# Counting stage of a graph kernel: TensorE reads the one-hot where VectorE wrote it, without ScalarE's copy to columns-first

## The reference, cut to what matters

```python
x = _layernorm(x + _L0_gnn_ref(x, edge_index, 6250), axis=-1)
x = _layernorm(x + _L1_gnn_ref(x, edge_index, edge_attr_40, edge_weight, ...), axis=-1)

# layer 0
row, col = edge_index with a self loop for each node
deg = segment_sum(ones, row)
norm = deg_inv_sqrt[row] * deg_inv_sqrt[col]
out = segment_sum(label_mat[row] * norm[:, None], col)

# layer 1
gate = silu(edge_attr @ W1.T + b1) @ W2.T + b2 + adapt_logit
msg = gate * h[dst] * (cw * node_mult[dst])[:, None]
agg = segment_sum(msg, src) / clip(segment_sum(node_mult[dst], src))
```

## Time and profile before

| | before |
|---|---|
| median of 3 runs | 3051.34 us (3043.43 to 3051.47) |
| the profiled execution's own time | 3027.21 us |
| its span, first to last instruction | 3025.4 us |
| mean granted TensorE clock | 0.850 |
| busy: TensorE matmul, VectorE, ScalarE, GpSimd | 74%, 79%, 46%, 70% |
| ScalarE's copy `by_col<-oh_hi` (L323) | x101, 178.7 us, mean 1794 ns |

### The profile page before, as it was taken

One profiled execution on the slowest core, in us unless ns is written; L12 is line 12 of the kernel. 1 busy time (PEld: TensorE's weight loads), 2 busy tenths in 40 slices (PEclk: granted clock), 3 DMA queues, 4 the chain that ended last, 5 costly groups with the idle time before them and its releaser, 6 DMA issues. The chain is left out here.

```text
span 3025.4 us, 73628 instructions
## 1 busy us (share of the span) xinstructions
PE 2250.1 (74%) x25909; PEld 1913.9 (63%) x25909; DVE 2404.3 (79%) x5424; ACT 1395.5 (46%) x2929; POOL 2121.9 (70%) x1852
## 2 busy tenths in 40 slices
PE   6980476678777787777787877787878787788475
PEld 5760365566666666655666666676767666667475
DVE  9994577777787777877788897888888878887698
ACT  7982244444444444444444444444444444445123
POOL 7506777877777777777777777777777777760165
PEclk9765688888888888988888898888989888979797
DMA  8405233333433434333344454444444444442896
GB/s 322 148 2 163 62 112 108 101 126 116 127 113 115 127 115 124 117 112 112 118 148 153 143 155 146 147 145 145 145 147 147 144 144 145 156 138 103 333 389 224
DMA packets 174987, 441.53 MB, mean 146 GB/s; under 512 B 92662, under 2 KB 92662, under 8 KB 154806
## 3 DMA queue, kind: packets, MB, share of 16 engines
q1 hardware_dynamic: 103754, 236.05, 23.4%
q0 software_dynamic: 67888, 194.98, 20.7%
q10 hardware_dynamic: 3004, 5.90, 0.6%
HBM read 292.51 MB, written 144.27 MB: 144 GB/s over the span
## 5 line engine op out<-in xcount | busy, mean ns | idle before, releaser
L722 POOL DMA_INDIRECT slot<-table,gidx x1616 | 1811.9, 1121 | 633.6 <-issue 620.2
L821 PEld LDWEIGHTS route<-parts,oh_r 128*128 128x128 bf16 x11312 | 764.9, 100 | 91.6 <-issue 66.9
L821 PE MATMUL route<-parts,oh_r 128*128 128x148 bf16 x11312 | 812.9, 232 | 3.2 <-DVE parts L1224 3.0
L1089 DVE TENSOR_SCALAR oh_r<-iota_r,spot 128x896 bf16<-128x896 f16 x1616 | 613.5, 451 | 74.4 <-PE route L821 74.4
L894 ACT ACTIVATE routed<-route 128x444 bf16<-128x444 f32 (+1 forms) x1010 | 507.9, 513 | 258.5 <-PE route L821 240.0
L856 PE MATMUL pwin<-slot,oh_d 128*128 128x144 bf16 x1616 | 167.6, 276 | 404.2 <-DMA slot<-table,gidx 372.1
L856 PEld LDWEIGHTS pwin<-slot,oh_d 128*128 128x128 bf16 x1616 | 147.8, 155 | 428.2 <-issue 270.0
L777 PEld LDWEIGHTS pwin<-win,oh_t 128*128 128x128 bf16 x4848 | 262.3, 117 | 200.6 <-issue 101.8
L777 PE MATMUL pwin<-win,oh_t 128*128 128x80 bf16 (+1 forms) x4848 | 277.0, 227 | 77.1 <-ACT ssum L904 71.6
L747 PE MATMUL phid<-attr,w 80*96 80x512 f32 x404 | 282.2, 789 | 44.4 <-issue 44.1
L1195 DVE TENSOR_TENSOR prod<-slot,got 128x256 f32<-128x256 f32 x202 | 84.6, 419 | 231.3 <-ACT parts L955 231.2
(11 more groups left out here) (228 smaller groups left out, 3257.3 us busy)
## 6 DMA issues: line engine op xcount, KB each, us to landing
rows<-slots SPq DMA_DIRECT2D x51, 1295.0 KB, 8.8
oh_t<-dst_row SPq DMA_DIRECT2D x101, 512.0 KB
erows<-slots SPq DMA_DIRECT2D x51, 777.0 KB
attr<-in_edge_attr SPq DMA_DIRECT2D x101, 320.0 KB
slots<-zeros SPq DMA_DIRECT2D x53, 518.0 KB
slot<-table,gidx POOLq DMA_INDIRECT x1616
table<-tab SPq DMA_DIRECT2D x3, 676.0 KB, 5.9
weight_t<-weights SPq DMA_DIRECT2D x101, 8.0 KB
```

What stands on the lines that cost most here:

```text
L722: e.indirect_dma_start(out=slot[:, s, g, :], out_offset=None, in_=table0, in_offset=bass.IndirectOffsetOnAxis(ap=gidx[:, s, g:g + 1], axis ...
L821: mm = e.matmul(route[:, (NPH * m + phase) % 2, RC * (j - a):RC * (j - a + 1)], oh_r[:, c, slot_of, :], parts[:, s % 2, c, :], start=(c == ...
L1089: oh = e.tensor_scalar(oh_r[:, c], iota_r[:, :, :], spot[:, s % 2, c:c + 1], None, ALU.is_equal)
```

## The change

`by_col`, its semaphore `laid` and ScalarE's step `lay` go. TensorE's step `count` waits for VectorE's `oh_ready` (both one-hots of the tile) and takes its moving operands from `oh_hi` itself: 51 columns with a step of 16 elements for `deg`, and for `tot` four runs of 52 columns, each with a step of 16 elements. The values that enter each sum are the same, and so are the outputs.

```diff
@@ ScalarE
-                    def lay(i, s):
-                        t = U * i + s
-                        e.wait_ge(oh_ready, 2 * (t + 1))
-                        if since(i, s, OR):
-                            e.wait_ge(oh_used, t - OR + 2)
-                        e.activation(by_col[:, s % OR], oh_hi[:, s % OR].rearrange("p b g -> p g b"), ACT.Copy
-                                     ).then_inc(laid, 1)
-                    over_tiles(e, NT, U, (lay, 0))
@@ TensorE
                     def count(i, s):
                         t = U * i + s
-                        e.wait_ge(laid, t + 1)
+                        e.wait_ge(oh_ready, 2 * (t + 1))
                         for g in range(G):
-                            e.matmul(deg[:, 0:NP2], oh_lo[:, s % OR, :, g], by_col[:, s % OR, g, 0:NP2],
+                            e.matmul(deg[:, 0:NP2], oh_lo[:, s % OR, :, g], oh_hi[:, s % OR, 0:NP2, g],
                                      start=False, stop=False, skip_group_check=True)
-                        by_class = by_col[:, s % OR].rearrange("p (k q) b -> p k q b", q=CC)
+                        by_class = oh_hi[:, s % OR].rearrange("p b (k q) -> p k q b", q=CC)
                         for q in range(CC):
                             mm = e.matmul(tot[0:NT], band[:, bass.ds(NT - 1 - t, NT)], by_class[:, :, q, :],
                                           start=False, stop=False, skip_group_check=True)
```

More of the change, by code:

```diff
@@ L213, in build @@
             oh_hi = sb("oh_hi", [P, OR, HB, G], BF16, ph)
-            by_col = sb("by_col", [P, OR, G, HB], BF16, ph)
             band = sb("band", [P, 2 * NT], BF16, ph)
@@ L253, in build @@
             (src_in, dst_in, wl, x_in, types_in, tready, tstored, types_got, qready, wz, io, blank, filled, keyed,
-             mapped, oh_ready, oh_used, laid, counted, xready, highs, rested, mids, lows, stored, v, g_own, a_own,
+             mapped, oh_ready, oh_used, counted, xready, highs, rested, mids, lows, stored, v, g_own, a_own,
              chunked, dst_done, rows_ok, cum_ok, bad_ok, fault_ok, rows_set, rows_turned) = (
@@ L257, in build @@
                                      "types_got", "qready", "wz", "io", "blank", "filled", "keyed", "mapped",
-                                     "oh_ready", "oh_used", "laid", "counted", "xready", "highs", "rested", "mids",
+                                     "oh_ready", "oh_used", "counted", "xready", "highs", "rested", "mids",
                                      "lows", "stored", "v_w", "g_own", "a_own", "chunked", "dst_done", "rows_ok",
```

## The result

The changed kernel takes 3167.3 us as the median of 4 runs (3164.5 to 3171.4), before 3047.4 (4 runs): the ratio is 1.0402, 95% interval 1.0374 to 1.0430, so 120 us or 4.0% slower. The forecast was 3185 us, 134 more. The profiled execution took 3164.47 us, with a span of 3162.7.

A forecast was written before the change was run, and what follows sets the result against it. The prediction took ScalarE's copy to set the counting's pace, 1.857 us a tile; TensorE's strided reads would make it 3.23, ending the counting at 349.0 us against 214.8. That adds 134 to 3051.3, giving 3185 us, range 3110 to 3215.

The forecast's parts named there:

- The bound before: Counting stage of the unchanged kernel: 1.857 us a tile, with ScalarE's copy of 1.79 us as the step setting the pace.
- VectorE's 1.70 us: Counting stage: VectorE's time for a tile where nothing holds it, taken as 1.70 from 1.64 to 1.73 us.
- The 64 ns are the strided weight load, not the array: Spacing of deg matmuls before: 64 ns at either clock, put down to reading oh_lo weights with a step of 32 bytes.
- A column costs 1.96 ns: TensorE's moving read of oh_hi at 32 bytes' step: 1.96 ns a column, taken from ScalarE's copy.
- the sum: TensorE's tile after the change: deg 1.60 plus tot 1.63, together 3.23 us, counting ending at 349.0 us.
- The whole time: Whole kernel after the change: 3051.3 + 134 = 3185 us, 4.4% slower.
- A time, not a ratio: Strided column price taken as 1.96 ns; the rival ratio, 2.3 times 0.41 ns, gave 0.95 ns and 3045 us, chance 0.06.
- the milder rival: TensorE's moving read: a lone column costs two accesses, 1.68 ns, so 2.77 us a tile and 3140 us; chance 0.22.
- The lower bound from L794: TensorE's moving read: a lone column costs 0.84 ns at 8 bytes' step, and 32 bytes is unlikely to be cheaper.
- The reads add up: Rival for deg matmuls: weight load and moving read follow one another, 164 ns each, 4.25 us a tile, 3286 us; chance 0.05.
- VectorE's wait takes the place of TensorE's: Counting stage: VectorE waits for TensorE to free oh_hi, some 1.5 us a tile, 140 us and more in all.

The follow-up runs named there:

- e7: Kernel before with contiguous weights (a tile of ones) for the deg matmuls: deg 27 ns apart, counting ended at 193.4 us, against 215.7.
- e10: Kernel after with oh_hi laid out at 4 bytes between a column's elements: 3015.1 us in one run, counting ended at 192.2 us.
- e12: The 4-byte oh_hi layout without the copy, run in more rounds: 3022.1 us against 3033.2 for the kernel before, ratio 0.9951.
- e6: Kernel after with contiguous weights (a tile of ones) for the deg matmuls: deg 95 ns apart, counting ended at 328.0 us.
- e8: Kernel after with 8 more dense 512-column matmuls of zeros a tile, to raise TensorE's clock: tot 375 ns at both clocks, counting ended at 619.8 us.
- the ladder: Moving reads of oh_hi at steps of 32, 16, 8 and 4 bytes compared: 1.80, 1.76, 0.89 and 0.45 ns a tot column.
- e4: Kernel after with oh_hi laid out at 8 bytes between a column's elements: ratio to before 0.9998, counting ended at 200.2 us.
- e2: Kernel before with only the four tot matmuls reading oh_hi directly, deg still reading by_col: ratio 1.0236.
- e1: Kernel before with only the 16 deg matmuls reading oh_hi directly, tot still reading by_col: ratio 1.0105, counting ended at 258.4 us.

## Why the prediction was right, point by point

- **The bound before.** The pace of 1.857 us was read rightly, but not what sets it: the prediction names ScalarE's copy, with 1.79 us, and that step does not set the pace. The mean length of a copy is not the pace of copies either: in e7 they take 1716 ns each and start 1634 apart. What sets the pace is the round trip of the ring of three, of which the prediction saw only the waits. One such trip, with TensorE's two rows at 154.98 and 156.00 in the earlier trace rows:

```profile
151.39 0.59 DVE L460 TENSOR_TENSOR oh_hi<-number,hi 128x832 bf16<-128x832 bf16 x1 [0.19 <-PE tot_bank L360]
151.89 1.22 DVE L463 TENSOR_TENSOR oh_lo<-number,lo 128x2048 bf16<-128x2048 bf16 x1
153.15 3.60 ACT L323 ACTIVATE by_col<-oh_hi 128x832 bf16<-128x832 bf16 x2 [0.17 <-DVE oh_lo L463]
...
157.06 0.59 DVE L460 TENSOR_TENSOR oh_hi<-number,hi 128x832 bf16<-128x832 bf16 x1 [0.21 <-PE tot_bank L360]
```

VectorE fills the buffer, ScalarE copies it, TensorE reads it, and VectorE writes it anew, three tiles later. In the mean over 95 tiles that is 1727 ns for VectorE, 1797 for the copy, 1758 for TensorE and 291 for the three handovers: 5573 ns, and a third of it is 1.858 us. In 86 of the 95 VectorE starts within 0.2 us of TensorE's end. In e7 the same sum is 1719 + 1716 + 976 + 291 = 4702 ns, a third of which, 1.57, is less than VectorE's 1.64, so VectorE sets the pace there. The misreading cost the prediction nothing, since the copy goes and TensorE alone needs more than all that; but it hid that before could be 22 us faster with its copy in place, if its weights had no step.

- **VectorE's 1.70 us.** It is 1.64 where nothing holds it (e10, e12). That changed nothing either, as TensorE is slower.
- **The 64 ns are the strided weight load, not the array.** Shown by e7 (27 ns without the step), and by the earlier trace rows at both clocks. No run varied the step of the weights, so how the 64 ns come about inside a load is not shown.
- **A column costs 1.96 ns.** The term that was off: 374 / 208 = 1.80 for `tot`, 8% less. That another engine's price came so near was luck in part, since ScalarE's copy was itself lengthened by TensorE's reads: from e7's 1716 ns it would be (1716 - 161) / 832 = 1.87. For `deg` 101 / 51 = 1.98, of which e6 gives 95 / 51 = 1.86 to the stream and 6 ns to the weight load beside it; the term was right there by two errors that cancel. The tile took 3.12 us where the sum had 3.23, and the counting ended at 339 and not 349. With the measured size the sum gives 29.2 + 99 x 3.12 = 338.
- **The whole time.** 3167 us where 3185 was forecast. Of the 18 us, 11 are the counting (123 lost and not 134), 4 the median of before, which came out at 3047.4 and not 3051.3, and the other 3 are within the scatter.
- **A time, not a ratio.** Shown by e8. For `tot` the milder rival's 1.68 ns was closer to the 1.80 than the forecast's 1.96, but its reason, two accesses of 0.84, is not what the ladder shows.
- **The lower bound from L794.** Its value held at a step of 8 bytes (0.89 ns in e4, against 0.84). Its reading as a price for each lone element did not: at 4 bytes it is 0.45 (e10). And that 0.84 came out was luck in part. In the trace of before the three matmuls behind the sum of 0.43 us start 215, 114 and 95 ns ahead of the next one at the high clock, and 427, 215 and 140 at the low one (medians; the low one has two of each kind), so the first two go with the array's clock and are not a time that stays the same at either. What the ladder supports is 1.8 ns for each 16 bytes touched, which is the line of 16 bytes of the Trainium skill ("SBUF — State Buffer", section "Specifications (TRN2)") with a price that the page does not give. That two hits on a line give the full bandwidth, as the same section says, the runs do not bear out for this read: at 8 bytes two columns share a line, and cost 0.89 ns each where contiguous ones cost 0.43 at the high clock.
- **The reads add up.** Out: 101 ns a `deg` matmul, not 164.
- **VectorE's wait takes the place of TensorE's.** Seen, 132 us at 95 tiles, where 140 and more was forecast. The later stages moved along; the second was 14 us longer in the profile, which one execution of it leaves open.

## What to carry to other kernels

Removing a copy that only changes a layout moves its awkward read to whoever reads next. Count how many elements that reader takes (here 1648 a tile instead of 832), and price them by a strided read in the trace as a time, not as a multiple of the reader's own speed: here the step of 32 bytes cost ScalarE 2.3 times its contiguous read, and TensorE 374 / 89 = 4.2 times at its high clock. Where buffers go round between engines, add up the round trip and divide it by their number before you name one engine as the bound. Before paying for a copy or doing without it, see whether the writer can put down another order for nothing: with 2 or 4 columns of the tile innermost the same elements, written at the same cost, made the copy needless, for a gain of 0.5% or so on two chips and none that showed on two others.

## What the runs showed of the hardware that was not expected

- TensorE's moving read of bf16 took 0.45, 0.89, 1.76 and 1.80 ns a column at steps of 4, 8, 16 and 32 bytes. At 8 bytes and more this is no faster than contiguous columns at the low clock (0.83 ns), even where the array has the high one.
- A strided read on one engine lengthened that of another: ScalarE's copy took 1716 ns with contiguous weights on TensorE (e7), 1794 with strided weights (before), 1840 and 1883 with strided weights and a strided moving operand (e2, e1).
- With a moving operand of 32 bytes' step TensorE was busy without a pause and still at its low clock. In the kernel after, that is the plain matmul of 0.63 us at 338.42. In e1 the granted clock of the windows reads 1.00:

```profile
100.00:105.00 5.00, 5.00 (x47) 1.00 0.17 56
```

but the contiguous `tot` matmuls there start 173 ns apart in the median, which is 208 columns at 1.2 GHz, and never 89. In the trace of before the same holds for the first 36 us: a window reads 1.00 and the four `tot` matmuls take 0.91 us, as at 0.50 in the earlier trace rows.

```profile
30.00:36.00 6.00, 5.01 (x59) 1.00 1.03 398
```

```profile
32.02 0.91 PE L360 MATMUL tot_bank<-by_col,band 128*101 128x208 bf16 x4
```

The traces' first record of the clock comes at 36 us in before and at 385 in e1. So ahead of the first record the column says 1.00 whatever the clock was; the spacing of plain matmuls is what to trust. In e4, with a step of 8 bytes (from 37 us on), and in e8, with dense matmuls between, the clock did rise. That the clock stays low is no part of the loss of the whole change, since the strided read has the same price at both (e8), but it is of e1's, where `tot` took 0.67 us and not 0.36.
